# A transformer block on one core: the shared gated unit moved behind the loop's periods, another order of steps, a compact last-key product

## The reference

```python
x1 = x + xattn(layernorm(x), ctx)      # 16 heads of 128, q and k rms-normed, 257 keys
x2 = x1 + attn(layernorm(x1))          # 16 heads of 16, 4 key/value heads, rotary, causal, ternary weights
xt = layernorm(x2)
probs = softmax(xt @ Wg); e = argmax(probs)         # one of 8 experts per token, 256 places each
routed = expert_e(xt) * gate                        # (silu(xt @ W1[e]) * (xt @ W3[e])) @ W2[e]
shared = silu(xt @ sw1) * (xt @ sw3) @ sw2          # for every token, hidden width 352
out = x2 + routed + shared
```

## Time and profile before

| | us |
|---|---|
| median of 3 runs | 1424.43 (1420.79 to 1424.91) |
| profiled execution | 1421.66, span 1419.8 |
| PE busy | 1270.2 (89%) |
| DVE busy | 916.5 (65%) |
| ACT busy | 884.8 (62%) |
| POOL busy | 574.4 (40%) |

### The profile page before, as it was taken

How to read it: one execution, slowest core, us unless ns; L and a number is a source line. 1 busy time by engine, 2 the same in 40 slices (tenths; PEclk the granted TensorE clock), 3 DMA queues, 4 the chain that set the end, 5 groups by cost and what they waited for, 6 DMA issues and landing times.

```text
span 1419.8 us, 34906 instructions
## 1 busy us (share of the span) xinstructions
PE 1270.2 (89%) x10526; PEld 853.6 (60%) x10526; DVE 916.5 (65%) x3313; ACT 884.8 (62%) x3728; POOL 574.4 (40%) x1371
## 2 busy tenths in 40 slices
...
PEclk9888999999999999999999999999999999996699
...
DMA packets 36130, 55.18 MB, mean 39 GB/s; under 512 B 6748, under 2 KB 29433, under 8 KB 35040
## 3 DMA queue, kind: packets, MB, share of 16 engines
...
q10 hardware_dynamic: 1056, 0.02, 0.0%
...
## 4 chain that ended last, share of the span: by engine, by line
PE 52%; DVE 17%; issue 9%; ACT 8%; POOL 4%; DMA 1%; POOLq 0%; DVEq 0%; ACTq 0%
PE AB L595 27%; PE Db L595 9%; PE Eb L595 7%; DVE kst L1351 3%; PE C L595 3%; DVE rq L1408 2%; PE C L720 2%; PE C L735 2%; POOL prob L1169 2%; ACT AB L946 2%; ACT prob L1014 2%; DVE pT L1538 2%; DVE px L1620 1%; ACT wt_q L938 1%; ACT rkb L1008 1%
## 5 line engine op out<-in xcount | busy, mean ns | idle before, releaser
L946 ACT ACTIVATE AB<-AB 128x128 f32<-128x128 f32 (+1 forms) x1160 | 303.3, 261 | 105.0 <-PE AB L595 101.7
L1124 POOL TENSOR_TENSOR pjunk<-pjunk 128x1 f32<-128x1 f32 x289 | 57.5, 199 | 681.4 <-DVE sinv L1533 386.4
L1351 DVE BATCH_NORM_STATS2 kst<-AB 128x6 f32<-128x256 f32 x512 | 181.7, 416 | 107.1 <-PE AB L595 102.0
L595 PE MATMUL AB<-wk_hi,c_hi 128*128 128x512 f16 x512 | 199.4, 389 | 19.1 <-POOL c_lo L1130 7.3
L946 ACT ACTIVATION_READ_ACCUMULATOR AB<-AB 128x1 f32 (+1 forms) x1160 | 215.6, 186 | 0.0
L595 PE MATMUL AB<-wk_lo,c_hi 128*128 128x512 f16 x512 | 197.8, 386 | 0.0
L595 PE MATMUL AB<-wk_hi,c_lo 128*128 128x512 f16 x512 | 197.7, 386 | 0.0
L1014 ACT ACTIVATE prob<-prob,nbias,rq 128x257 f32<-128x257 f32 x256 | 150.6, 591 | 8.4 <-DVE nbias L1528 8.4
L1169 POOL TENSOR_SCALAR prob<-prob,sinv 128x257 f32<-128x257 f32 x256 | 129.7, 507 | 20.2
L595 PE MATMUL AB<-ctxT,qpT 128*128 128x257 f32 x512 | 123.2, 383 | 11.5 <-ACT pxT L1046 11.5
L595 PEld LDWEIGHTS AB<-wk_hi,c_hi 128*128 128x128 f16 x512 | 50.9, 99 | 101.2 <-issue 29.3
...
## 6 DMA issues: line engine op xcount, KB each, us to landing
...
ctxn<-in_ctxn SPq DMA_DIRECT2D x64, 128.0 KB, 2.1
...
xin<-in_x SPq DMA_DIRECT2D x16, 128.0 KB, 2.2
...
xres<-in_x SPq DMA_DIRECT2D x16, 128.0 KB, 2.1
out<-base SPq DMA_DIRECT2D x16, 128.0 KB, 1.7
...
```

What stands on the lines that cost most here:

```text
L595: return pe.matmul(out, lhsT, rhs, start=start, stop=stop)
L946: ins = nc.scalar.activation(k, k, ACT.Square, accum_out=sums[0:m, h:h + 1])
L1124: own.mark(pool.tensor_tensor(pjunk[:, 0:1], pjunk[:, 1:2], pjunk[:, 1:2], ALU.mult))
L1351: ins = V.bn_stats(stats[:, 0, 2 * half + n], AB[0:m, 2 + half, 2 * D * n:2 * D * (n + 1)])
```

## The change

Four things.

1. The shared unit leaves the periods. A period now stores its halfway result `x2` into the output and its turned norm `xn2T` into scratch memory (`store_halfway` on SP, two stores where there was one). In the last period all 16 tiles' units follow: `U0` to `U15` (up, sigmoid, hidden) and `D0` to `D15` (down, sum), which load `xn2T` and `x2` back (four buffers each), and store the sum. They stand between the steps of tile 15's late part, and the rest of them behind it. Their banks alternate between 0/1, 2/3 and 4/5. The experts' rows are loaded behind `D9`.
2. All engines have a new order of steps in the periods (`ORDER`), and the last period has its own (`LAST_ORDER`).
3. The last-key product: `plast` holds 12 columns instead of a diagonal of 4 x 12, PE makes one product of 12x128 instead of four, and ACT writes the four groups of `pTl` by four copies of 12x128 with a scale of 0 or 1 per row (`own_group`) instead of one copy of 12x512.
4. Three kinds of DVE instruction with per-row scalars become forms with two tensors (`layer_norm`, `step_rq`, the one-hot).

```diff
 ORDER = {
-    "PE": "K0 pt3 K1 X K2 o3 K3 f Q xt1 K4 qkv QP rk0 s0 qk sc rk1 K5 K6 K7 pt0 pv s1 st pr rk2 s2 o0 xt2 rk3
-              lg up s3 pt1 dn pos o1 pt2 o2"
-    "ACT": "K0 tl3 K1 X ph3 K2 oh3 K3 gKN0 Q xt1 gRQ K4 qkv gqkv QP rk0 qk e0 rk1 K5 sc K6 K7 ph0 gKN1 pv tl0
-              rk2 e1 xt2 rk3 oh0 up e2 ph1 lg tl1 e3 oh1 ph2 tl2 oh2"
-    "DVE": "K0 X K1 XL dp3 K2 K3 KN0 do3 kn0 f Q RQ K4 rq qkv qr s0 sc K5 i0 sm K6 K7 KN1 dp0 kn1 ys yv s1 pr
-              ln2 i1 s2 do0 lg up s3 i2 dn dp1 pos do1 dp2 i3 do2"
-    "POOL": "h0 n3 h1 X h2 c0 c1 r0 cl ln1 r1 h3 n0 r2 y r3 ln2 c2 n1 c3 n2 scat"
+    "PE": "K0 pt3 K1 X K2 o3 K3 f Q xt1 K4 qkv rk0 QP s0 qk sc rk1 K5 K6 K7 pt0 pv s1 pr st rk2 s2 o0 xt2 rk3 s3 lg
+              pt1 pos o1 pt2 o2"
+    "ACT": "K0 K1 ph3 X tl3 K2 oh3 K3 gKN0 Q xt1 gRQ K4 qkv gqkv QP rk0 qk e0 K5 sc K6 rk1 K7 ph0 gKN1 pv tl0 e1 rk2
+              oh0 xt2 rk3 e2 ph1 lg tl1 e3 oh1 ph2 tl2 oh2"
+    "DVE": "K0 X K1 XL dp3 K2 K3 KN0 do3 kn0 f Q RQ rq qkv K4 qr s0 sc i0 K5 sm K6 K7 KN1 dp0 kn1 ys s1 yv pr ln2 i1
+              s2 do0 s3 i2 lg dp1 pos i3 do1 dp2 do2"
+    "POOL": "h0 n3 h1 X h2 ln1 c3 r0 c0 r1 h3 n0 c2 cl r2 y r3 ln2 n1 c1 n2 scat"
...
+LAST_ORDER = {
+    "PE": "U0 pt3 U1 o3 f D0 U2 xt1 D1 qkv U3 D2 qk sc U4 D3 pv U5 st pr D4 U6 xt2 lg D5 U7 pos D6 U8 D7 U9 D8 U10 D9
+             U11 D10 U12 D11 U13 D12 U14 D13 U15 D14 D15"
...
+            def store_halfway(p):
+                sp.wait_ge(drained["E"].sem, drained["E"].at(p, "pr"))
+                sp.dma_start(d["out"][bass.ds(p.tile * P, P), :], x2[:]).then_inc(x2_out.sem, 16)
+                sp.wait_ge(drained["D"].sem, drained["D"].at(p, "xt2"))
+                sp.dma_start(turned_rows[bass.ds(p.tile * P, P), :], xn2T[:].rearrange("p k n -> p (k n)")).then_inc(xn2T_out.sem, 16)
...
+            for n in range(TILES):
+                s = BANK_PAIRS[n][1]
+                sp.wait_ge(filled[s].sem, filled[s].at(LAST, f"U{n}"))
+                if n + 4 < TILES - 1:
+                    load_turned(n + 4)
+                sp.wait_ge(drained["E"].sem, drained["E"].at(LAST, f"D{n}"))
+                sp.dma_start(d["out"][n * P:(n + 1) * P, :], back_of(n)).then_inc(sum_out[n % 4] if n < TILES - 1 else last_out, 16)
+                if n + 4 < TILES - 1:
+                    sp.wait_ge(sum_out[n % 4], 16 * (n // 4 + 1))
+                    load_back(n + 4)
+                if n == 9:
+                    load_rows()
...
-                for g in range(G):
-                    ins = mm(Db[0:LK, P * g:P * (g + 1)], plast[:, b, g], ident16[:])
-                ins.then_inc(filled["D"].sem, 1)
+                mm(Db[0:LK, 0:P], plast[:, b], ident16[:]).then_inc(filled["D"].sem, 1)
...
+            def last_probs(p, b):
+                act.wait_ge(filled["D"].sem, filled["D"].at(p, f"pt{b}"))
+                for g in range(G):
+                    ins = nc.scalar.activation(pTl[0:LK, b % 2, P * g:P * (g + 1)], Db[0:LK, 0:P], ACT.Copy,
+                                               scale=own_group[0:LK, g:g + 1])
...
-                V.tensor_scalar(out, x, mv[:, 0:1], rstd[:, n:n + 1], ALU.subtract, ALU.mult).then_inc(xn_ready.sem, 1)
+                V.scalar_tensor_tensor(out, x, mv[:, 0:1], rstd[:, n:n + 1].broadcast_to([P, DIM]), ALU.subtract, ALU.mult)
...
+            def shared_sum(p, n):
+                dve.wait_ge(filled["E"].sem, filled["E"].at(p, f"D{n}"))
+                if n < TILES - 1:
+                    dve.wait_ge(back_in[n % 4], 16 * (n // 4 + 1))
+                V.tensor_tensor(back_of(n), back_of(n), Eb[:, 0:DIM], ALU.add).then_inc(drained["E"].sem, 1)
```

More of the change, by code:

```diff
@@ L137, in settle @@
             self.seen = self.n
-LATE = {"n3", "ph3", "tl3", "oh3", "pt3", "o3", "dp3", "do3", "f", "ln1", "xt1", "qkv", "qr", "gqkv", "qk", "sc", "sm", "pv", "ys", "st", "yv", "y", "pr",
-        "ln2", "xt2", "lg", "up", "pos", "dn", "scat"}
 ORDER = {
-    "PE": """K0 pt3 K1 X K2 o3 K3 f Q xt1 K4 qkv QP rk0 s0 qk sc rk1 K5 K6 K7 pt0 pv s1 st pr rk2 s2 o0 xt2 rk3
-              lg up s3 pt1 dn pos o1 pt2 o2""".split(),
-    "ACT": """K0 tl3 K1 X ph3 K2 oh3 K3 gKN0 Q xt1 gRQ K4 qkv gqkv QP rk0 qk e0 rk1 K5 sc K6 K7 ph0 gKN1 pv tl0
-              rk2 e1 xt2 rk3 oh0 up e2 ph1 lg tl1 e3 oh1 ph2 tl2 oh2""".split(),
-    "DVE": """K0 X K1 XL dp3 K2 K3 KN0 do3 kn0 f Q RQ K4 rq qkv qr s0 sc K5 i0 sm K6 K7 KN1 dp0 kn1 ys yv s1 pr
-              ln2 i1 s2 do0 lg up s3 i2 dn dp1 pos do1 dp2 i3 do2""".split(),
-    "POOL": """h0 n3 h1 X h2 c0 c1 r0 cl ln1 r1 h3 n0 r2 y r3 ln2 c2 n1 c3 n2 scat""".split(),
+    "PE": """K0 pt3 K1 X K2 o3 K3 f Q xt1 K4 qkv rk0 QP s0 qk sc rk1 K5 K6 K7 pt0 pv s1 pr st rk2 s2 o0 xt2 rk3 s3 lg
+              pt1 pos o1 pt2 o2""".split(),
+    "ACT": """K0 K1 ph3 X tl3 K2 oh3 K3 gKN0 Q xt1 gRQ K4 qkv gqkv QP rk0 qk e0 K5 sc K6 rk1 K7 ph0 gKN1 pv tl0 e1 rk2
+              oh0 xt2 rk3 e2 ph1 lg tl1 e3 oh1 ph2 tl2 oh2""".split(),
+    "DVE": """K0 X K1 XL dp3 K2 K3 KN0 do3 kn0 f Q RQ rq qkv K4 qr s0 sc i0 K5 sm K6 K7 KN1 dp0 kn1 ys s1 yv pr ln2 i1
+              s2 do0 s3 i2 lg dp1 pos i3 do1 dp2 do2""".split(),
+    "POOL": """h0 n3 h1 X h2 ln1 c3 r0 c0 r1 h3 n0 c2 cl r2 y r3 ln2 n1 c1 n2 scat""".split(),
+}
+BANK_PAIRS = ["01", "23", "01", "23", "45"] + ["01", "23"] * 6
+LAST_ORDER = {
+    "PE": """U0 pt3 U1 o3 f D0 U2 xt1 D1 qkv U3 D2 qk sc U4 D3 pv U5 st pr D4 U6 xt2 lg D5 U7 pos D6 U8 D7 U9 D8 U10 D9
+             U11 D10 U12 D11 U13 D12 U14 D13 U15 D14 D15""".split(),
+    "ACT": """tl3 ph3 U0 oh3 U1 xt1 U2 qkv gqkv U3 qk sc U4 pv U5 xt2 U6 lg U7 U8 U9 U10 U11 U12 U13 U14 U15""".split(),
+    "DVE": """dp3 U0 do3 f U1 D0 qkv U2 D1 qr U3 D2 sc sm U4 D3 ys yv pr ln2 U5 D4 lg U6 D5 pos U7 D6 U8 D7 U9 D8
+              U10 D9 U11 D10 U12 D11 U13 D12 U14 D13 U15 D14 D15""".split(),
+    "POOL": """n3 ln1 y ln2 scat""".split(),
 }
@@ L415, in build @@
         slot_ready = Events(sem("slot_ready"), full=["h"], last=["h"])
[L416 to L417 removed]
+        sig_ready = Events(sem("sig_ready"), last=[f"U{n}" for n in range(TILES)], expert=["h"])
+        sig_exp = Events(sem("sig_exp"), last=[f"{k}{n}" for n in range(TILES) for k in "el"], expert=["e", "l"])
         scattered = Events(sem("scattered"), 16, pro=["zeros"], full=["scat"], last=["scat"])
@@ L448, in build @@
         ew13 = [x[:, 0:KC * 2 * FC * P].rearrange("p (k w f) -> p k w f", k=KC, w=2) for x in spare]
+        turned = [x[:, KC * 2 * FC * P:KC * 2 * FC * P + DIM].rearrange("p (k n) -> p k n", k=KC) for x in spare]
+        back = [x[:, KC * 2 * FC * P + DIM:KC * 2 * FC * P + 2 * DIM] for x in spare]
         rkx_words = rkx[:].rearrange("p a k n -> p (a k n)")
@@ L1058, in root_guess, with step_xt2 @@
                 nc.scalar.activation(guess[name][:], guess[name][:], ACT.Exp, scale=-0.5).then_inc(guess_ready.sem, 1)
+            def step_xt2(p):
+                act.wait_ge(xn2T_out.sem, xn2T_out.before(p))
+                drain(p, "xt2", "D", flat2(xn2T), Db[:, 0:DIM])
             def step_qk(p):
```

168 lines of the change are left out of this document (106 added, 62 removed).

## The result

The changed kernel takes 1429.4 us in the median (1421.7 to 1436.8, 20 runs) beside 1424.6 of the kernel before (1420.3 to 1426.8, 20 runs): ratio 1.0035, interval 1.0019 to 1.0050. It is slower by a third of a per cent, where 1380 us were forecast. The profiled execution took 1433.7 us, in the upper part of the 20 runs; its span is 1431.9 us at a mean granted clock of 0.951 (before 1419.8 at 0.962).

The account below looks back on a forecast made before the run. PE was taken to bound the loop's periods, while it stands still in the last period. Profiled 1421.7 - 61.5 (loop) - 0.5 (prologue) + 19.4 (tail) = 1379; median forecast 1380 us, range 1356 to 1402.

Parts of the forecast that it names:

- The loop: 15 periods: 5.28 us of work leaves PE in each, 1.2 is given back, so 4.1 us a period, 61.5 us gained.
- The forecast's own case: Whole kernel: the prediction's main sum holds, with a time of 1366 to 1390 us; chance 0.61.
- Rival B: Loop clock: two PE waits 4 us apart bring one 1.2 GHz stretch a period, 14 us more, 1394 us; chance 0.13.
- over 74.4 is D: Sign set beforehand: a period over 74.4 us, against 71.6 forecast, would show that Rival D holds.
- What the waits give back: Loop: ACT becomes the engine everyone waits for at a period's end; 1.2 of 5.3 us a period are given back.
- the list: Hand-laid order of a period's steps on all engines from block 1's scores on, with a time for each.
- The tail: After the last full period: the shared units set into tile 15's chain and behind it add 19.4 us.
- Prologue: Before the loop: its four last-key products take 0.5 us less.
- Forms at nothing: DVE's norms as two-tensor forms: 1.2 us of DVE saved a period, counted as nothing since DVE isn't the bound.
- Rival C: Tail: SyncE's queue of store, wait and load paces the units at 5 us each, 9 us more, 1389; chance 0.07.
- Rival D: Loop: ACT's row of steps decides the period, making the kernel slower than before, 1431 us; chance 0.06.
- Rival A: Loop: the waits give almost nothing back, so 5.3 to 5.9 us gained a period, 1357 us; chance 0.13.

Follow-up runs that it names:

- experiment 8: Changed kernel plus 22 useless PE products a period and tag writes spread one a period: 1384.8 us; also with old last-key product 1384.6, with old order 1411.8.
- experiment 9: Changed kernel with 17 useless products a period and tag writes spread: 1383.5 us; kernel before with seven useless products and tag writes spread: 1409.9 us.
- experiment 4: Changed kernel with the periods' old order of steps on all four engines, the last period's order left new: 1430.2 us, ratio 1.0051 to the kernel before.

## Why the prediction was wrong, by its own steps

The median was missed by 49 us (1429.4 against 1380), the profiled execution by 54.7 (1433.7 against 1379). By stretches of that execution:

- **The loop, +47.8.** Forecast: 76.05 - 4.1 = 71.95 us a period in the mean; measured 75.14.
  - **The clock, 36 us: this is the step that failed.** The forecast's own case put the clock at nothing beyond the four falls that were there. Rival B, which I gave 0.13, had the mechanism and the wrong size: it took one fall a period at 1.3 us, 14 us, and there came two, which together cost 75.14 - 72.73 = 2.4 us a period. I took rows at 1.00 as the loop's clock without asking how near to a fall it was. The sign that I had set didn't lead there either: "over 74.4 is D", and 75.14 was the clock. In the period shown PE has six waits of 0.6 to 1.4 us, the longest 0.2 us longer than the longest before. The Trainium skill (TensorE: Matmul & The Clock Gate, A second HAM failure mode: psum-queue depth-cycling) tells of a kernel whose clock goes back and forth because PE idles briefly and often between groups of matmuls. The trace agrees: 28 falls in a loop in which PE never waits longer than 1.4 us at once. Beside that section B should have had more than 0.13.
  - **"What the waits give back", 12 us.** 1.2 us a period were given back by the list. With the clock held in both kernels it was 2.4 (75.65 - 5.28 + 2.4 = 72.8, against 72.73), and 0.4 of the falls before went (76.05 to 75.65), which the forecast had left in: 2.4 - 1.2 - 0.4 = 0.8, times 15. Some 0.5 of the 2.4 are probably the useless products' own, since new-order periods with neither fall nor product take 72.1 to 72.3; then 38 us are the clock's (beyond the falls that the forecast had left in) and 10 the waits'. Two waits were not in the list, `QP` behind `K4`'s statistics and the last-key product behind `lgs`. ACT's last-key copies took 1.10 us a block where 0.8 was set, and PE waits for them at `pos`; that this is why the compact product gave nothing in the end (experiment 8) fits, but wasn't tried by itself. The new order was right in its direction: about 1 us a period (experiment 8).
- **The tail, +8.2.** Forecast +19.4, measured +27.6. The pause of 9.5 us ahead of `sc` is all of it: without the row of tag writes the tail is 170.3 to 171.8 us in six traces, where 151.7 + 19.4 = 171.1 was forecast. I had read the 1.39 us pause of the earlier trace rows (issue) inside `sc` as a constant. It goes with the row too (experiment 9), and nothing in the sum asked what lay beside it. That 171.1 fits so well is partly luck: it contains what the row cost in the one trace that the base was read from. With the row spread in both kernels the tail grows from 149.1 to 171.0, by 21.9 us and not 19.4. The units behind `pos` took 3.98 us each (4.1 forecast), the experts 69.3 (69.2; that 5% of 72.4 is 3.6 and not 3.4 changes nothing).
- **Prologue, -1.3** beyond the forecast. **Forms at nothing**: right. **Rival C** (SyncE's queue): one wait of 0.6 us for a load; it does not pace the tail. **Rival D**: its time (1431) was met and its cause wasn't: with the clock held the period is 72.7 on the same row of steps. ACT's part is inside the 2.4 us. **Rival A**: falls with the 2.4.

The sum: 47.8 + 8.2 - 1.3 = 54.7.

What stays open: the row of tag writes is shown to be the pause's cause, by moving and by spreading it; how it holds up the other engines isn't. That it holds up the loading of new code is argued. For it: two, then one engine stand with their inputs there, the place follows the row of small writes and not the step, and the units' data transfers are hardly needed. The Trainium skill (Runtime: NRT & Kernel Launch, Instruction fetch mechanics) has the engines load code in blocks of 16 KiB by DMA and calls the cost mostly hidden; the transfers of that size in the trace last 0.9 to 2.0 us elsewhere, 2.8 (at 1273.4) beside the row, and 3.0 beside the row in the kernel before. Against it: none recorded lasts the 8 us of the pause, and with the row moved no transfer of the instruction queues is recorded from 1307 to 1338 us, while PE stood still for 5.2 us at 1318.5. Nor is it settled which of PE's waits calls a fall. Neither their sum nor the longest decides: in the period of experiment 4 without a fall PE's waits sum to 6.0 us, the longest 2.2, against 5.8 and 1.4 with two falls. And the useless products both fill waits and give PE more to do; the two weren't told apart.
